# Shared expert of a two-layer decoder: sequences 2 to 7 in three pairs, a pair signalled once per product

## The reference

```python
scores = jax.nn.softmax(xf @ gate_w.T, axis=-1)
_, idx = jax.lax.top_k(scores + gate_b, K)          # K = 6 of E = 64
...
xb = jnp.zeros((E, CAP, D), xf.dtype).at[se, pos].set(xf[tok], mode='drop')   # CAP = 64
h = jax.nn.silu(jnp.einsum('ecd,eid->eci', xb, w1)) * jnp.einsum('ecd,eid->eci', xb, w3)
yb = jnp.einsum('eci,edi->ecd', h, w2)
...
y = jnp.zeros_like(xf).at[tok].add(contrib * wf[:, None])
z = jax.nn.silu(xf @ ws1.T) * (xf @ ws3.T) @ ws2.T  # the shared expert, hidden width 176
return (y + z).reshape(shape)
```

## Time and profile before

| | us |
|---|---|
| median of 3 runs | 1830.53 |
| lowest and highest run | 1821.31, 1835.14 |
| profiled execution, first to last instruction (span) | 1863.1 |
| TensorE busy in the span | 1624.9 |
| VectorE busy in the span | 1105.7 |
| ScalarE busy in the span | 824.0 |

### The profile page before, as it was taken

One profiled execution on the slowest core, in us unless ns is written; L12 is line 12 of the kernel. 1 busy time (PEld: TensorE's weight loads), 2 busy tenths in 40 slices (PEclk: granted clock), 3 DMA queues, 4 the chain that ended last, 5 costly groups with the idle time before them and its releaser, 6 DMA issues.

```text
span 1863.1 us, 41690 instructions
## 1 busy us (share of the span) xinstructions
PE 1624.9 (87%) x17616; PEld 1059.5 (57%) x17616; DVE 1105.7 (59%) x2233; ACT 824.0 (44%) x1516; POOL 241.0 (13%) x403
## 2 busy tenths in 40 slices
PE   4898988999874878998998998998998998998985
PEld 2655555555543754674665665665665665665663
DVE  5277777777561346386386377277277376376354
ACT  1555565555511114345345445435435435435422
POOL 1011110111024510011011011011011011011011
PEclk9999999999976879999999999999999999999998
DMA  8512111111157240011011011010010011001000
GB/s 279 196 47 69 50 58 53 52 63 45 51 152 63 80 145 23 19 40 35 17 42 35 2 57 35 2 58 30 6 58 29 8 40 47 7 1 49 5 1 6
DMA packets 65001, 95.71 MB, mean 51 GB/s; under 512 B 9431, under 2 KB 47297, under 8 KB 64083
## 3 DMA queue, kind: packets, MB, share of 16 engines
q1 hardware_dynamic: 61491, 89.20, 14.5%
q0 software_dynamic: 2560, 3.46, 2.2%
q10 hardware_dynamic: 768, 0.40, 0.1%
HBM read 56.03 MB, written 38.80 MB: 51 GB/s over the span
## 4 chain that ended last, share of the span: by engine, by line
PE 55%; DVE 24%; issue 7%; ACT 7%; POOL 4%; DMA 1%; another core or an unknown queue 1%; ACTq 0%; DVEq 0%; SPq 0%; POOLq 0%; PEldq 0%
PE psum L994 6%; DVE peak L1285 5%; PE psum L808 5%; PE psum L902 5%; ACT prob L1162 3%; PE psum L649 3%; PE psum L664 3%; PE psum L889 3%; PE psum L674 3%; DVE w_shared L1285 3%; PE psum L860 2%; PE psum L817 2%; POOL rstd L1462 2%; PE psum L803 2%; DVE kx L1412 1%
## 5 line engine op out<-in xcount | busy, mean ns | idle before, releaser
L1162 ACT ACTIVATE prob<-psum 128x1024 f32<-128x1024 f32 (+1 forms) x352 | 322.7, 945 | 350.4 <-PE psum L797 107.5
L1285 DVE TENSOR_REDUCE w_shared<-psum 128x4 bf16<-128x1024 f32 (+1 forms) x160 | 194.1, 1223 | 187.8 <-PE psum L713 123.2
L1285 DVE TENSOR_REDUCE peak<-psum 128x4 bf16<-128x1024 f32 (+1 forms) x160 | 190.5, 1216 | 15.6 <-PE psum L738 11.9
L1459 POOL TENSOR_TENSOR rstd<-moments,eps 128x2 f32<-128x2 f32 x64 | 15.4, 241 | 1006.7 <-DVE moments L1207 1006.7
L808 PE MATMUL psum<-qt,kt 64*128 64x256 f32 x1024 | 131.4, 376 | 0.0
L902 PE MATMUL psum<-prob,v_big 128*64 128x256 f32 x1024 | 124.6, 385 | 0.2 <-issue 0.2
L808 PEld LDWEIGHTS psum<-qt,kt 64*128 64x128 f32 x1024 | 98.5, 189 | 10.9
L902 PEld LDWEIGHTS psum<-prob,v_big 128*64 128x64 f32 x1024 | 68.0, 136 | 42.9 <-issue 11.9
L943 PE MATMUL psum<-prob,va 128*32 128x256 f32 (+1 forms) x1536 | 88.1, 354 | 1.1 <-ACT prob L1162 0.8
L1313 DVE TENSOR_TENSOR qt<-qt,psum 128x1024 f32<-128x1024 f32 x32 | 38.3, 1216 | 84.7 <-PE psum L970 84.7
L1106 ACT ACTIVATE kt<-psum,b_qk 128x256 f32<-128x256 f32 x128 | 53.7, 470 | 51.3 <-PE psum L664 50.9
(11 more groups left out here) (330 smaller groups left out, 3254.5 us busy)
## 6 DMA issues: line engine op xcount, KB each, us to landing
zd<-kx SPq DMA_DIRECT2D x24, 512.0 KB, 5.9
union<-zd SPq DMA_DIRECT2D x16, 768.0 KB, 4.4
w_late<-ad SPq DMA_DIRECT2D x16, 512.0 KB, 3.8
w_late<-vd SPq DMA_DIRECT2D x16, 512.0 KB, 4.7
ad<-union SPq DMA_DIRECT2D x16, 256.0 KB, 2.2
vd<-union SPq DMA_DIRECT2D x16, 256.0 KB, 2.3
xg<-union SPq DMA_DIRECT2D x16, 192.0 KB, 2.0
w_late<-in_w1T SPq DMA_DIRECT2D x1, 2816.0 KB
```

The source lines that it names most:

```text
L1162: nc.scalar.activation(prob_of[a][s][:, slot + 2 * i:slot + 2 * i + 2, 0:n], v.pair(step, i)[:, :, 0:n], ACT.Exp, scale=a.scale).then_inc( ...
L1285: nc.vector.tensor_reduce(dst, src, axis=AX.X, op=ALU.max).then_inc(v.free(step), 1)
```

## The change

Sequences 2 to 7 are done as three pairs ahead of the experts. A pair's F1 is eight matmuls in two pairs of banks, (1, 5) and (2, 3); banks 2 and 3 are also used by UP, later. It signals `f_h_full` once, by 4. A pair's F2 is twelve matmuls in the two halves of bank 7 and signals `f_z_full` once, by 2. ScalarE, VectorE and the sync queue do both sequences of a pair in turn. Sequences 0, 1 and 8 to 15 stay single. Sequence 8 and F2 of 6 and 7 stand ahead of chunk 0's UP, sequence 9 and F2 of 8 beside chunk 1, none beside chunks 2 and 3. `LAST_STEPS` stays 10.

```diff
--- before.py
+++ after.py
@@ -1585,11 +1585,11 @@
         f_act = [flat(t[0:FI, :, :]) for t in vx]
         f_hid = [t[0:FI, 0:512].rearrange("p (i t) -> p i t", i=2) for t in va]
         F_STORES = (range(0, 7), range(7, 12), range(12, 14), range(14, 16))
-        BEFORE_EXPERTS = 5
-        LAST_STEPS = BEFORE_EXPERTS + CHUNKS + 1
+        TWOS_END = 8
+        LAST_STEPS = TWOS_END + CHUNKS - 2
         f_store = [p for p, seqs in enumerate(F_STORES) for _ in seqs]
 
-        XT_BANK, UP_BANKS, Y_BANK, F_BANKS, Z_BANK = 0, (2, 3, 4), 6, (1, 5), 7
+        XT_BANK, UP_BANKS, Y_BANK, F_BANKS, Z_BANK = 0, (2, 3, 4), 6, ((1, 5), (2, 3)), 7
 
         merged = sem("merged")
         sort_link = sem("sort_link")
@@ -1618,19 +1618,23 @@
 
         def expert_steps():
 
-            rest = iter(range(1, SEQS))
+            rest = iter([(0, 1), (1, 1)] + [(c, 2) for c in range(2, TWOS_END, 2)] + [(c, 1) for c in range(TWOS_END, SEQS)])
+            last = [next(rest)]
 
             def shared(n):
                 out = []
                 for k in [k for _, k in zip(range(n), rest)]:
-                    out += [("F1", k), ("F2", k - 1)]
+                    out += [("F1", *k), ("F2", *last[0])]
+                    last[0] = k
                 return out
 
-            out = [("F1", 0), ("merge", 0)] + shared(1) + [("slots", 0)] + shared(BEFORE_EXPERTS)
+            out = [("F1", *last[0]), ("merge", 0)] + shared(1) + [("slots", 0)] + shared((TWOS_END - 2) // 2)
             for c in range(CHUNKS):
-                beside = shared(1 if c < CHUNKS - 1 else 0)
-                out += [("XT", c, 0), ("XT", c, 1)] + beside[:1] + [("UP", c), ("DOWN", c, 0)] + beside[1:] + [("DOWN", c, 1)]
-            return out + shared(SEQS) + [("F2", SEQS - 1)]
+                beside = shared(1 if c < CHUNKS - 2 else 0)
+                early = 1 if c else 2
+                out += ([("XT", c, 0), ("XT", c, 1)] + beside[:early] + [("UP", c), ("DOWN", c, 0)] + beside[early:]
+                        + [("DOWN", c, 1)])
+            return out + shared(SEQS) + [("F2", *last[0])]
 
         def experts_tensor(pe):
             mm = nc.tensor.matmul
@@ -1652,22 +1656,24 @@
                 elif kind == "F1":
                     if c:
                         pe.wait_ge(f_h_ready, c)
-                    for i in range(4):
-                        last = mm(psum[0:FI, F_BANKS[i // 2], 256 * (i % 2):256 * (i % 2) + 256], ws13[:, i, :], tokens_t[c],
-                                  start=True, stop=True)
-                        if i == 1:
-                            last.then_inc(f_h_full, 1)
-                    last.then_inc(f_h_full, 1)
+                    for j in range(step[2]):
+                        for i in range(4):
+                            last = mm(psum[0:FI, F_BANKS[j][i // 2], 256 * (i % 2):256 * (i % 2) + 256], ws13[:, i, :],
+                                      tokens_t[c + j], start=True, stop=True)
+                            if i == 1 and step[2] == 1:
+                                last.then_inc(f_h_full, 1)
+                    last.then_inc(f_h_full, 1 if step[2] == 1 else 4)
                 elif kind == "F2":
-                    pe.wait_ge(f_h_ready, c + 1)
                     if c:
                         pe.wait_ge(f_z_out, c)
-                    for t in range(2):
-                        z, rows = psum[:, Z_BANK, 128 * t:128 * t + 128], slice(128 * t, 128 * t + 128)
-                        for i in AB:
-                            mm(z, f_hid[c % 2][:, i, rows], ws2[:, i, :], start=(i == 0), stop=False)
-                        last = mm(z, tokens_t[c][:, rows], ident[:, :], start=False, stop=True)
-                    last.then_inc(f_z_full, 1)
+                    for j in range(step[2]):
+                        pe.wait_ge(f_h_ready, c + j + 1)
+                        for t in range(2):
+                            z, rows = psum[:, Z_BANK, 256 * j + 128 * t:256 * j + 128 * t + 128], slice(128 * t, 128 * t + 128)
+                            for i in AB:
+                                mm(z, f_hid[(c + j) % 2][:, i, rows], ws2[:, i, :], start=(i == 0), stop=False)
+                            last = mm(z, tokens_t[c + j][:, rows], ident[:, :], start=False, stop=True)
+                    last.then_inc(f_z_full, step[2])
                 elif kind == "XT":
                     if step[2] == 0:
                         pe.wait_ge(gathered[c], 16 * NB)
@@ -1713,11 +1719,13 @@
             for step in expert_steps():
                 kind, c = step[0], step[1]
                 if kind == "F1":
-                    act.wait_ge(f_h_full, 2 * c + 1)
-                    nc.scalar.activation(f_act[c % 2], psum[0:FI, F_BANKS[0], :], ACT.Tanh, scale=0.5).then_inc(f_tanh, 1)
+                    for j in range(step[2]):
+                        act.wait_ge(f_h_full, 2 * c + (1 if step[2] == 1 else 4))
+                        nc.scalar.activation(f_act[(c + j) % 2], psum[0:FI, F_BANKS[j][0], :], ACT.Tanh, scale=0.5).then_inc(f_tanh, 1)
                 elif kind == "F2":
-                    act.wait_ge(f_z_full, c + 1)
-                    nc.scalar.copy(tokens_t[c], psum[:, Z_BANK, 0:256]).then_inc(f_z_out, 1)
+                    act.wait_ge(f_z_full, c + step[2])
+                    for j in range(step[2]):
+                        nc.scalar.copy(tokens_t[c + j], psum[:, Z_BANK, 256 * j:256 * j + 256]).then_inc(f_z_out, 1)
                 elif kind == "XT":
                     act.wait_ge(e_xt_full, 2 * c + step[2] + 1)
                     nc.scalar.copy(e_xt[c % 2][:, 512 * step[2]:512 * step[2] + 512], psum[:, XT_BANK, :]).then_inc(
@@ -1787,16 +1795,18 @@
                     linked(ts(slot_key, slot_key, float(TOPK), None, ALU.mult))
                     linked(tt(z_row, slot_key, slot_lo, ALU.add))
                 elif kind == "F1":
-                    h1, h3 = [psum[0:FI, b, :] for b in F_BANKS]
-                    hid = flat(f_hid[c % 2])
-                    dve.wait_ge(f_tanh, c + 1)
-                    if c >= 2:
-                        dve.wait_ge(f_z_full, c - 1)
-
-                    fused(hid, f_act[c % 2], 1.0, h1, ALU.add, ALU.mult).then_inc(f_link, 1)
-                    dve.wait_ge(f_link, c + 1)
-                    dve.wait_ge(f_h_full, 2 * c + 2)
-                    fused(hid, hid, 0.5, h3, ALU.mult, ALU.mult).then_inc(f_h_ready, 1)
+                    for j in range(step[2]):
+                        k = c + j
+                        h1, h3 = [psum[0:FI, b, :] for b in F_BANKS[j]]
+                        hid = flat(f_hid[k % 2])
+                        dve.wait_ge(f_tanh, k + 1)
+                        if k >= 2:
+                            dve.wait_ge(f_z_full, k - 1)
+
+                        fused(hid, f_act[k % 2], 1.0, h1, ALU.add, ALU.mult).then_inc(f_link, 1)
+                        dve.wait_ge(f_link, k + 1)
+                        dve.wait_ge(f_h_full, 2 * c + 2 * step[2])
+                        fused(hid, hid, 0.5, h3, ALU.mult, ALU.mult).then_inc(f_h_ready, 1)
                     if c >= LAST_STEPS:
                         prepare_tables(c - LAST_STEPS)
                 elif kind == "XT" and step[2] == 0:
@@ -1859,9 +1869,10 @@
             for step in expert_steps():
                 kind, c = step[0], step[1]
                 if kind == "F2":
-                    sp.wait_ge(f_z_out, c + 1)
-                    sp.dma_start(xz[c * T:c * T + T, :].rearrange("(t p) w -> p t w", p=128),
-                                 tokens_t[c].rearrange("p (t w) -> p t w", t=2)).then_inc(f_stored[f_store[c]], 16)
+                    for k in range(c, c + step[2]):
+                        sp.wait_ge(f_z_out, k + 1)
+                        sp.dma_start(xz[k * T:k * T + T, :].rearrange("(t p) w -> p t w", p=128),
+                                     tokens_t[k].rearrange("p (t w) -> p t w", t=2)).then_inc(f_stored[f_store[k]], 16)
                     if c == LAST_STEPS - 1:
                         sp.wait_ge(p1.fold_kept, 128 * ITERS)
                         sp.wait_ge(e_h_full, 4 * CHUNKS)
```

## The result

The changed kernel takes 1836.26 us (median of 10 runs, 1827.34 to 1842.62), the kernel before 1828.11 us in the same session (10 runs, 1820.13 to 1836.99). The ratio is 1.0045, interval 1.0023 to 1.0067: 8.2 us slower, 4 to 12. The prediction said 1843, 13.5 us slower than before, and gave "within 1%" a chance of 0.67.

What follows compares the result with a forecast made beforehand. The prediction took TensorE, busy 87% of the span, as the bound; 6 (overlap) + 2.5 (cover) + 5 (clock) = +13.5 us on 1830.5 gave 1844, rounded to 1843 us, range 1815 to 1858.

Steps and rivals of the forecast that it cites:

- Step 1: Ahead of the experts, pairs lose overlap: TensorE idles while VectorE's products finish before the next F1; +6.2 us, taken as 6.
- Step 2: Beside the experts, chunks 0 and 2 lose cover: idle time before chunk 2's UP and both second DOWNs; +2.5 us.
- Step 3: In the pairs' stretch, idle times drop TensorE's granted clock to half in three stretches; +5 us.
- Step 4: Over three pairs, F1 and F2 give 12 fewer signals; taken as 0 us.
- Step 5: Sync and GpSimd queues: stores and gathers cost 0; gathers do not hide the loss, which stays lost ahead of the tail.
- The premise: Stage between attention phases: timed runs are mostly without the profile's hole, 27 us of idle TensorE awaiting a late signal.
- B: Between the attention phases: the hole is real and pairs cross it, UP starting earlier; -18.7 us, 1812 us, chance 0.12.
- C: The hole is real, both kernels sit in it until gathers end; -1 or +13 us by held signal, 1836, chance 0.18.
- D: Ahead of the experts: the clock stays low from the first idle time until UP; +26 us, 1856 us, chance 0.15.

Runs made afterwards that it cites:

- two pairs: Changed kernel with sequences 2 to 5 paired, 6 single, 7 to 9 beside the chunks as before; ratio to the kernel before 0.9978, run again 0.9998.
- cover for chunk 3: Kernel before with F1 of sequence 10 and F2 of 9 moved beside the last chunk; 1870.03 us, ratio 0.9997.
- spaced pairs: Changed kernel with each later chunk's gathers issued only after the previous chunk's transposes signalled; 1853.51 us, ratio 1.0145 to the kernel before.
- filler run: Changed kernel with 15 more matmuls, five in each idle place, results unread; 1876.45 us, ratio 1.0033 to the kernel before.

## Why the prediction was right, and where it was not

**Step 1, overlap lost (forecast +6.2): right in the trace.** Idle times of 2.51, 2.88, 0.79 and 0.99 us are 7.17 us. The kernel before has 0.33 and 0.68 in their place in the trace without a hole, so 6.2 us more. The single values were forecast as 2.2, 2.9 and 1.8. UP was forecast 35.7 us behind F1 of sequence 2 (582.3 less 546.6, with the clock's 5 us) and came after 33.5. The step's own check has a slip: its terms for UP of the kernel before add up to 568.0, not 567.0, and one F2 of 1.42 us in them is too many. Without it they give 566.6, as in the trace without a hole (19.9 us behind F1 of sequence 2).

**Step 2, cover beside the experts (+2.5): right in this trace, too low on the chips with the hole.** The predicted idle times stand at 591.58, 607.49 and 614.68, of 0.95, 0.68 and 0.95 us. From F1 of sequence 2 to chunk 3's second transposes the changed kernel needs 617.04 - 550.93 = 66.1 us. The kernel before, put together from its 564.43 - 546.74 = 17.7 us and three chunks of 12.22 us, needs 54.4. That is 11.8 us more (before rounding), the 9.0 ahead of UP and 2.8 behind it. But timed alone the placement cost 5.6 us (2 to 9). Its trace says what stands beside the idle times: from F2 of sequence 5, behind the hole, to the first transposes of the next phase it takes 109.8 us, the kernel before 103.1, and the clock was half in chunks 2 and 3. All five profiles with this placement and the hole have a granted clock of 0.50 from 640 to 650 us, in chunk 2 or at the head of chunk 3. The four with the hole and with work beside chunk 2 (the one before the prediction, the kernel before again, two pairs, cover for chunk 3) have 0.94 to 1.00 there. The prediction's clock term counts the pairs alone and has nothing for this. In the changed kernel's own profile the clock stayed at 1.00 in the chunks, so it is no part of the 11.8 us; in the run with spaced pairs, without a hole, it was 0.50 from 605 to 640.

**Step 3, the clock (+5): the mechanism right, the size too large in this trace.** F1 took 5.37 and 5.04 us instead of 3.69, together 3.0 us. I had assumed three low stretches with half of 3.4 us of work lost in each; there were two, none behind the third idle time (0.99 us). In the run with spaced pairs there were three, the third behind 1.00 us: the three F1 lost 1.6, 3.0 and 1.1 us, together 5.7. So the term differs between executions by about as much as it was off, and 5 lies between the two. That filler matmuls gave F1 its 3.69 us back shows the cause.
The Trainium skill, TensorE: Matmul & The Clock Gate, section "What's actually happening", has the clock released by TensorE's activity and throttled without it; the filler run agrees (3.69 us instead of 5.37), while the half-clock stretch behind 0.68 us of idle time in the two-pair run has no idle time that explains it.

**Step 4, fewer signals (0): not refuted.** One signal per sequence shortened an idle time by 0.95 us, by overlap; no run shows a price of the signal itself.

**Step 5, queues (0): right for the gathers.** In the changed kernel the transposes of chunk 0 did not wait for rows. When gathers were put off the waits came at once, 12.37 us in the run with late ones. The same step says that what is lost ahead of the tail stays lost, and that was not tested. GpSimd's 32 gathers and 32 scatters take 80.4 us from the first start to the last even when it never waits (564.14 to 644.57), and the sync queue loads the scattered rows 82.6 us after the first gather there (646.71). In four of the five profiles without a hole, the changed kernel's among them, the last thing that this load waited for was the scatters and not TensorE; the two-pair run is the fifth. The first gather starts 1.4 us behind F1 of sequence 2, so the kernel before without a hole would have that load some 84 us behind this F1 (an estimate from these two numbers); the changed kernel has it after 90.4. By that only some 6 of the 11.8 us reach the next phase, fewer if the last scatter lands as late as in the changed kernel (6.0 us after its start, against 2.1). This is argued: no profile shows the kernel before without a hole.

**The sum.** 13.5 forecast, 11.8 on TensorE's path, 8.2 measured (4 to 12). The step that missed most in that trace is the third, by 2 us. The remaining 3.6 us between trace and times are within the interval, but the two-pair kernel says that more is involved. Its trace shows 5.06 us more idle time ahead of the chunks than the kernel before, and low clock besides, 9.6 us to UP in all. Yet it was as fast as the kernel before (0.9998, -3.8 to +3.3 us) on one chip and no slower (0.9978) on another. So in timed runs most of what the change costs came with the third pair and the placement, and two pairs cost little or nothing. Slack behind GpSimd's scatters, as under step 5, would be one reason; it would not be enough alone, since by the same reckoning two pairs should cost some us too. Another would be the clock: a half-clock stretch like that of chunk 3 above makes about 5 us, and comes in some executions only; if fewer of them fall on a kernel that has had its idle time earlier, that would balance the pairs. Both are argued, not shown: with one profile of each kernel no run counts such stretches.

**The premise.** The sum rested on the timed runs being without the hole, and for the runs of the result this held: the changed kernel's profile has none and matches its timed runs to the microsecond (1836.03 in a median of 1836.26). The reason that I weighed, a hole made by recording, fell, so that the premise held was in part luck: on a chip of the other kind the base of the sum would have been off by 42 us, and the ratio would have come out about the same (1.0039) for other reasons. There are two levels of the same program: 1828 us where none of the five profiles has a hole, and 1870 us on two other chips, where all eight have one. Each chip was used at one time only, so chip and moment are not told apart. By its hole and its length the trace shown before the prediction (span 1863.1) is of the second kind; the times beside it are of the first. That is why it looked like an artefact. The rule of the Trainium skill, NOTIFIC — the notification-queue block, section 7.1, about a recorder that holds back its producers, explains nothing here, since timed runs are as long as profiled ones on both kinds.

**Rivals.** B (pairs cross the hole, 1812) did not come about: where there is a hole, the pairs sit in it. C is what happens at the 1870 us level, with the worse of its two held signals; the change costs 7 us there, inside C's -1 to +13. The runs of the result are of the other kind. D (clock low until UP, 1856) did not come about either: in the changed kernel's profile F1 of 6 and 7 was the last to be slow, and F1 of 8 took 1.96 us.

**Open.** What holds TensorE's signals for some 20 to 35 us on some chips. It goes with the gathers in time, but on the other kind of chip the same gathers, equally dense, hold nothing; and the runs meant to part gathers from signals fell on a chip without a hole. Whether spaced gathers would pay at the 1870 us level was therefore not measured. No version was measured clearly faster than the kernel before: the two-pair one cannot be told from it.

## What to carry to other kernels

A pair that signals once trades the neighbour's work for an idle time, and its size can be read off before: the other engine's whole work on the pair, less what TensorE has beside it; here 2.51 and 2.88 us against 2.2 and 2.9 forecast. More buffers or a signal per item take most or part of it back (2.9 to 0.76 us, 2.51 to 1.56), and a filler keeps the clock up over it. None of these shows in the time while a later wait ends by itself. Work that is moved away from beside a stage can also leave that stage at half clock, which costs more than the idle times that open up: read the granted clock of the stage as well as its waits. When a profile is longer than the timed runs by the size of one hole, profile the kernel a second time on another chip before deciding that the hole isn't real.

## What was unexpected of the hardware

- TensorE's signals reached ScalarE and VectorE up to 35.0 us late on two chips, with a hold of 20 us or more in each of the eight profiles, while 32 indirect gathers were issued 1.25 us apart. On the other chips the gathers ran at the same pace and no signal was late. The kernel before took 1870 us on the two chips, and 1828 on the others.
- The clock fell to half behind idle times of 2.51 us, and stayed full behind 1.56 us in the run with a signal per sequence. Behind 0.99 us it stayed full and behind 1.00 us it fell, in two executions of the same instructions. It also fell once in the middle of a chunk, with no idle time longer than 0.68 us.
- Behind the hole, from 640 to 650 us (chunk 2 or the head of chunk 3), the clock was 0.50 in all five profiles without F1 and F2 beside chunk 2, and 0.94 to 1.00 in all four with them.
